# A graph layer, a linear-attention mix and a feed-forward part: four input buffers for the node tiles, slot numbers read early, source terms ahead of the sums

## The chip, the cores and the metric

The kernel runs on one core of a Trainium2 chip. The metric is device time in microseconds (us). Before the change it is 3642.68 us, the median of 3 runs (3634.11 to 3653.83).

## The reference

For 6250 nodes with 256 features, and 206,250 edges sorted by destination:

```python
xn = layernorm(x)
# graph attention, H=8 heads of D=32, T=4 edge types, F=16 edge features
feat_src = (xn @ W_n).reshape(N, H, D)
el = einsum('nhd,hdt->nht', feat_src, attn_l); er = einsum('nhd,hdt->nht', feat_src, attn_r)
em = einsum('ef,hft->eht', edge_attr_16, attn_m)
e = leaky_relu((el[src] . mask + er[dst] . mask + em . mask) / 3)      # mask = edge_attr_4, summed over t
a = exp(e - segment_max(e, dst)[dst]);  a = a / segment_sum(a, dst)[dst]
rst = segment_sum(feat_src[src] * a, dst)
# linear attention over all nodes
q, k, v = split(xn @ Wqkv);  q = softmax(q, over features) * scale;  k = softmax(k, over nodes)
mix = layernorm(((k^T v) q) @ Wout) * gamma
x = x + rst + mix
# 8 experts: router weights from the mean over the nodes, two hidden layers with batch norm and relu
x = x + ffn(layernorm(x))
```

## The kernel before, in words

All arithmetic that matters here is float32. The engines run in parallel and wait for one another by semaphores; the order of work on each engine is written out by hand. Names: PE is the matrix engine, DVE, ACT and POOL work on vectors, SP only issues transfers; transfers from one queue are issued in the order of the code. A register load (`value_load`) reads a number from memory into a register of the engine's sequencer, which then addresses a buffer or sets the value of a wait.

**The node part** (`phase_nodes`, from L108) takes the nodes in 49 tiles of 128. The helper `tiles` (L89) writes the first five steps out, then lets a hook run (`between`), and then either loops over pairs of tiles or, with `unrolled=True`, writes the rest out. A stage given with a lag works on an earlier tile in the same step. Its stages are:

1. Norm and node projection, about 11 to 200 us. SP loads a tile of x into `xin` (`load_x`, L242; two buffers, and from the third tile on it waits until `xn` of two tiles before is out). The load of tile 1 is followed by four tables of the edges' destinations (808 KB each) and the groups' first nodes. DVE takes statistics (`measure`, L434) and one tile later makes `xn` (`norm`, L441), with ACT making the standard deviation in between. PE transposes `xn` (L605), ACT copies it to `xq`, PE projects it (L618), ACT copies the result into `trow`, and POOL stores this row of the table in memory (`store_table`, L331). After tile 4 DVE derives the tables of the edge part (`edge_tables`, L449), 29.75 to 38.7 us. Once all 49 loads are issued SP issues the late weights (L271), the source indices `pidx`, the stores of the derived tables (L277 to L284) and 11 small stores for the table of visits (L286 to L291), most of them of 4-byte elements, one to a partition.
2. Projection to q, k and v, 223 to 345 us, PE bound. ACT copies the results (L403 to L405), DVE keeps the maximum of k. Meanwhile POOL gathers rows of the table for the first edges (`gather_ahead`, L346: 8 gathers of 128 rows each, then the store of the group). It does so for PRE_FIRST = 8 groups, waits for the maximum of k (L361), reduces it (L362), and gathers on up to PRE = 22 groups.
3. The context matrix and the mixed weights (345 to 425), then the mix itself, tile by tile (425 to 560). SP reloads x (`reload`) and stores the result (`store_mix`, L305). DVE runs `measure_out` (L563) for one tile and `finish` (L570) for the tile before, in each step `finish` first.

**The edge part** (`phase_edges`, from L694; about 580 to 2662 us) goes over the edges in K = 125 steps of two visits. A visit is a group of 1024 edges (8 chunks of 128) against one tile of 128 destination nodes. POOL gathers the source rows of a group into one of GSLOTS = 7 slots; which slot a visit uses is a number in memory (`vslot`), and how many groups must have landed is another (`vready`). `pairs` (L777) runs the steps, five written out, then a loop, then the last ones and some beyond the end, in which what is left of the last visits is done. What is done for step k:

- SP (L850) loads the inputs of step k+4 and stores the accumulators of the visits of step k-2, first visit ahead of the loads, second behind.
- PE (L1213): `turn_logits(k)` (L1178, transposes of e), one-hot turn of visit 0 of step k+1 (L1141), `edge_terms(k+1)` (L1149 and L1154, into ps_z), segment sums of visit 0 of step k-1 (L1201), the three register loads `slots_of(k+1)` (L1161, L1162), one-hot turn of visit 1, five chunks of the sums of visit 1, `turn_maxima(k)` (L1188), the other three chunks, `source_terms(k+1)` (L1168, into ps_z, after a wait for the gathered rows).
- DVE (L1083): `logits(k)` (L998: ps_z times the mask), the check for absent segments (`absent`), `over_terms` (L1006, the sum over t), the maxima of the visits, `leak` (L1012, gives e), new maxima of the accumulators (L1033, L1037), `messages(k-1)` for both visits (L1050 register load, L1053 multiply), two scans for the segment maximum (L1061, L1066), `join` of visit 0 of step k-2 (L1044: adds the new sums to the accumulator that ACT has rescaled), the one-hots of step k+2 (L992), `differences(k)` (L1072, L1073), `join` of visit 1.
- ACT takes the segment sums out of PE's buffer (L927), rescales the accumulators (L936) and makes the exponentials.

So ps_z goes from PE to DVE, e back to PE, its transposes to DVE's scans, the scanned maxima back to PE, and their transposes back to DVE.

**The feed-forward part** (`phase_ffn`, 2686 to 3649 us) isn't touched.

## Time and profile before

| what | before |
| --- | --- |
| median of 3 runs | 3642.68 us |
| profiled execution, its own time | 3650.95 us |
| its span | 3649.3 us |
| mean granted clock of TensorE | 0.921 of full |
| PE busy | 84% |
| DVE busy | 74% |
| ACT, POOL busy | 46%, 45% |
| data moved | 486.85 MB, mean 133 GB/s |

PE's busy share is an average: under 70% in most of the node part's slices and over 80% in the edge and feed-forward parts. Busy time is the sum of what the instructions took, so it says nothing of whether they were waited for. In rows of the trace in time, the bracket at the end gives the idle time of the engine ahead of the instruction and what ended it; "issue" is idle time in which the engine waited for nothing that the profile shows. A name with q behind it (DVEq, PEldq) is that engine's sequencer. Matmuls and their weight loads are two rows of one instruction (PE and PEld).

### The profile page before, as it was taken

To read this page: it belongs to the slowest core of one execution; us is meant where nothing else is said; L and a number is where in the kernel's file an instruction comes from. 1 tells how busy PE (TensorE), PEld (TensorE's weight loads), DVE (VectorE), ACT (ScalarE), POOL (GpSimd) and SP (SyncE) were. 2 spreads that over 40 slices of the span, in tenths; PEclk is the share of its full clock that TensorE was granted. 3 is DMA by queue.
4 is the path that set the end of the run, shared out by engine and by line. 5 is a ranking of instruction groups with operands and counts; after the bars stand their busy time and mean duration, and the time that the engine had idled before them with its cause. 6 is when DMAs were issued, how large, how long until landed. Compare 5 with 4: busy or idle time off the path is not lost. (4 is left out here: it accounts for less than half of the span.)

```text
span 3649.3 us, 78668 instructions
## 1 busy us (share of the span) xinstructions
PE 3076.3 (84%) x21479; PEld 2467.3 (68%) x21480; DVE 2687.0 (74%) x5071; ACT 1685.7 (46%) x5779; POOL 1632.3 (45%) x1744
## 2 busy tenths in 40 slices
PE   5469664888888888888888888888849999999999
PEld 2245443767676766767676767666637888888888
DVE  3346563888888888888888888888858776777776
ACT  2334221555555555555555555555533333333333
POOL 1144745766666666666766667777500000000000
PEclk7889876999999999999999999999969999999999
DMA  2253775766666666666666666666521000010000
GB/s 98 80 163 109 239 241 162 193 178 190 176 181 180 184 181 179 181 174 184 180 187 174 181 179 182 179 180 184 132 69 56 28 18 19 20 35 19 18 10 14
DMA packets 364693, 486.85 MB, mean 133 GB/s; under 512 B 165873, under 2 KB 268672, under 8 KB 358798
## 3 DMA queue, kind: packets, MB, share of 16 engines
q0 software_dynamic: 88032, 303.93, 29.3%
q1 hardware_dynamic: 276398, 180.19, 17.1%
q14 instruction: 192, 1.57, 0.1%
q8 instruction: 71, 1.16, 0.1%
HBM read 400.20 MB, written 83.68 MB: 133 GB/s over the span
## 5 line engine op out<-in xcount | busy, mean ns | idle before, releaser
L875 POOL DMA_INDIRECT gat<-scratch_table,idx x1440 | 1391.9, 967 | 638.0 <-issue 447.7
L1201 PE MATMUL ps_s<-msg,oh 128*128 128x272 f32 x4000 | 1012.9, 402 | 25.2 <-ACT tmp L927 15.2
L1201 PEld LDWEIGHTS ps_s<-msg,oh 128*128 128x128 f32 x4000 | 734.8, 191 | 160.8 <-ACT tmp L927 22.2
L1053 DVE TENSOR_TENSOR msg<-gat,ps_m 128x2048 f32<-128x2048 f32 x250 | 560.7, 2284 | 91.3 <-issue 91.3
L1457 ACT ACTIVATE h<-ps_h,fsh,fsc 128x512 f32<-128x512 f32 (+1 forms) x416 | 290.8, 750 | 567.1 <-PE ps_h L1642 567.1
L936 ACT ACTIVATE acc<-acc,sc 128x33 f32<-128x33 f32 x2000 | 458.9, 340 | 165.0 <-DVE acc L1044 165.0
L1422 POOL DMA_DIRECT2D out<-y x12 | 9.1, 761 | 927.2 <-DVE y L1597 927.2
L916 ACT CAST oh<-ps_o 128x1024 f32<-128x1024 bf16 x250 | 259.2, 1037 | 353.2 <-PE ps_o L1141 348.1
L927 ACT ACTIVATE tmp<-ps_s,sc 128x33 f32<-128x33 f32 x2000 | 384.4, 304 | 17.2
L1178 PE MATMUL ps_e<-ident,e 128*16 128x128 f32 x1000 | 149.4, 299 | 258.4 <-DVE e L1012 258.4
L1497 DVE CAST h_hi<-h 128x1024 fp32r<-128x1024 f32 (+1 forms) x208 | 137.4, 660 | 241.7 <-ACT h L1457 241.5
L1178 PEld LDWEIGHTS ps_e<-ident,e 128*16 128x16 f32 x1000 | 84.5, 94 | 327.6 <-DVE e L1012 309.1
L1066 DVE TENSOR_TENSOR_SCAN runm<-penr,ps_e 16x1024 f32<-16x1024 bf16 x125 | 284.3, 2275 | 12.8
L1061 DVE TENSOR_TENSOR_SCAN ps_e<-penr,ps_e 16x1024 f32<-16x1024 bf16 x125 | 284.5, 2276 | 2.0 <-PE ps_e L1178 2.0
L921 ACT ACTIVATE sc<-dd 128x16 f32<-128x16 f32 x250 | 60.0, 240 | 414.1 <-DVE dd L1037 400.2
L1499 DVE TENSOR_TENSOR h_lo<-h,h_hi 128x1024 fp32r<-128x1024 f32 (+1 forms) x208 | 242.1, 1164 | 7.1
L1640 PE MATMUL ps_y<-w_hi,h_hi 128*128 128x256 f32 x784 | 219.7, 280 | 1.4 <-DVE y L1597 1.4
L1641 PE MATMUL ps_y<-w_lo,h_hi 128*128 128x256 f32 x784 | 219.6, 280 | 0.0
L1642 PE MATMUL ps_y<-w_hi,h_lo 128*128 128x256 f32 x784 | 219.3, 280 | 0.0
L1149 PE MATMUL ps_z<-bdm,a 128*128 128x256 f32 x500 | 209.1, 562 | 0.0
L352 POOL DMA_INDIRECT stage<-scratch_table,pidx x176 | 173.9, 988 | 77.5 <-issue 51.7
L1141 PE MATMUL ps_o<-identb,ohT 128*128 128x128 bf16 x2000 | 184.4, 246 | 25.7 <-DVE ohT L992 24.2
(191 smaller groups left out, 5437.7 us busy)
## 6 DMA issues: line engine op xcount, KB each, us to landing
d16r<-scratch_dst SPq DMA_DIRECT2D x250, 256.0 KB
scratch_acc<-acc SPq DMA_DIRECT2D x250, 136.0 KB, 2.5
scratch_ahead<-stage POOLq DMA_DIRECT2D x22, 1152.0 KB, 4.9
gat<-scratch_ahead POOLq DMA_DIRECT2D x22, 1152.0 KB
gat<-scratch_table,idx POOLq DMA_INDIRECT x1440
a<-in_a SPq DMA_DIRECT2D x250, 64.0 KB
scratch_table<-trow POOLq DMA_DIRECT2D x49, 144.0 KB, 2.0
am<-scratch_acc SPq DMA_DIRECT2D x12, 544.0 KB, 4.0
```

Source lines behind the costliest of these rows:

```text
L875: pool.indirect_dma_start(out=gat[:, s, c, :], out_offset=None, in_=scr["table_rows"], in_offset=bass.IndirectOffsetOnAxis(ap=idx[:, g * C ...
L916: act.copy(oh[:, s, j, :, :], ps_o[:, 0:C, :]).then_inc(oh_ok, 1)
L927: act.mul(tmp[:, j, cols], ps_s[j][:, cols], sc[:, j, 1, h:h + 1]).then_inc(tmp_ok, 1)
L936: act.mul(acc[:, new, cols], acc[:, old, cols], sc[:, j, 0, h:h + 1]).then_inc(scaled, 1)
L1053: dve.tensor_tensor(m4[:, :, :, 0:DH], gat[:, row_of(at), :, 0:D].rearrange("p a c (h d) -> p (a c) h d", h=H), ps_p.rearrange("p (c j h) ...
L1061: dve.tensor_tensor_scan(ps_e[0:2 * H, 0:GE], penr[:, s, 0:GE], ps_e[0:2 * H, 0:GE], NEG, ALU.add, ALU.max).then_inc(runf_ok, 1)
L1066: dve.tensor_tensor_scan(runm[:, ::-1], penr[:, s, GE:0:-1], ps_e[0:2 * H, GE - 1::-1], NEG, ALU.add, ALU.max).then_inc(runm_ok, 1)
L1178: last = pe.transpose(ps_e[0:2 * H, c * P:(c + 1) * P], e[:, c * 2 * H:(c + 1) * 2 * H], ident[:, :])
L1201: last = pe.matmul(ps_s[j][:, 0:SUMS], oh[:, s, j, c, :], msg[:, 2 * (s % 2) + j, c, :], start=(c == 0), stop=(c == C - 1), skip_group_che ...
L1457: act.activation(hid[:, m, 0:n * P], ps_h[2 * layer + m][:, 0:n * P], ACT.Relu, bias=sh[:, layer, x * KD + m:x * KD + m + 1], scale=sc[:, ...
L1499: dve.tensor_tensor(lo, whole, hi.bitcast(F32), ALU.subtract).then_inc(parts, 1)
L1640: pe.matmul(out, a_hi, b_hi, start=start, stop=False)
```

## The change

In the node part: `xin` gets four buffers, SP loads x tile 0 ahead of the weights, and its loads are written out with the tables, the late weights, the derived tables and the visit stores put between them after tiles 3, 23 and 35. DVE's tiles of that stage are unrolled. `xn` moves to another region of memory. PRE becomes 24 and PRE_FIRST 11. In the mix DVE does `measure_out` ahead of `finish`. In the edge part: DVE reads both slot numbers at the start of a step; `join` of visit 1 moves from the end of step k to step k+1, behind `over_terms`; the stores on SP follow, and DVE and SP run one step more. PE reads its three numbers behind the first one-hot turn and does the source terms right behind the edge terms, ahead of all sums.

```diff
@@ -40,8 +40,9 @@
 K = V // 2
 SLOTS = 4
 GSLOTS = 7
-PRE = 22
-PRE_FIRST = 8
+PRE = 24
+PRE_FIRST = 11
+XB = 4
 BEFORE = 5
 NEG = -1.0e30
 SLOPE = 0.2
@@ -141,8 +142,7 @@
             wcat = early.enter_context(nc.sbuf_tensor("wcat", [P, KD, D + 2 * HT], F32))
             wnT = early.enter_context(nc.sbuf_tensor("wnT", [P, KD, D], F32))
             bd = early.enter_context(nc.sbuf_tensor("bd", [P, KD, 2 * HT], F32))
-            xin = early.enter_context(nc.sbuf_tensor("xin", [P, 2, D], F32))
-            xn = early.enter_context(nc.sbuf_tensor("xn", [P, 2, D], F32))
+            xin = early.enter_context(nc.sbuf_tensor("xin", [P, XB, D], F32))
         mixw = sb("mixw", [P, KD, D])
         qT = sb("qT", [P, 2, KD, P])
         xre = sb("xre", [P, 2, D])
@@ -170,6 +170,7 @@
         qsum = sb("qsum", [P, 2, H])
         qrs = sb("qrs", [P, NT, H])
         pidx = sb("pidx", [P, PRE * C], I32)
+        xn = sb("xn", [P, 2, D])
         stage = sb("stage", [P, 2, C, ROW])
 
         ps_tr = [ps(f"ps_tr{i}", [P, KD, P]) for i in range(2)]
@@ -185,7 +186,7 @@
         pool_step = sem("n_pool_step")
         attn_w = sem("n_attn_w")
         attn_wc = sem("n_attn_wc")
-        x_in = [sem(f"n_x_in{i}") for i in range(2)]
+        x_in = [sem(f"n_x_in{i}") for i in range(XB)]
         stats = sem("n_stats")
         var_ok = sem("n_var_ok")
         std = sem("n_std")
@@ -239,20 +240,13 @@
 
         @block.sync
         def _(sp):
-            def load_x(t, s):
-
-                if later(t):
-                    sp.wait_ge(xn_ok, t - 1)
-                sp.dma_start(xin[:, s, :], io["x"][row_of(t), :, :].rearrange("a p n -> (a p) n")) \
-                    .then_inc(x_in[s], 16)
-                if isinstance(t, int) and t == 1:
-
-                    for dst, name in ((d_em, "dst_em"), (dn_em, "dst_next_em"), (d_lin, "dst_lin"),
-                                      (dp_lin, "dst_prev_lin")):
-                        sp.dma_start(dst[:, :], io[name].rearrange("(p n) -> p n", p=P)).then_inc(dst_in, 16)
-                    sp.dma_start(gf[:, :], io["group_first"].rearrange("(a n) -> a n", a=1).broadcast_to([P, G - 1])) \
-                        .then_inc(dst_in, 16)
-
+            def load_x(t):
+
+                if t >= XB:
+                    sp.wait_ge(xn_ok, t - XB + 1)
+                sp.dma_start(xin[:, t % XB, :], io["x"][t]).then_inc(x_in[t % XB], 16)
+
+            load_x(0)
             sp.dma_start(wnT[:, :, :], io["W_nT"].rearrange("(c p) n -> p c n", p=P)).then_inc(weights_in, 16)
             sp.dma_start(wcat[:, :, 0:D], io["W_n"].rearrange("(c p) n -> p c n", p=P)).then_inc(weights_in, 16)
             sp.wait_ge(zeroed, 1)
@@ -261,12 +255,19 @@
                 for side, name in enumerate(("attn_l", "attn_r")):
                     sp.dma_start(bd[rows, h // 4, HT * side + T * h:HT * side + T * h + T],
                                  io[name][h]).then_inc(blocks_in, 16)
-            tiles(sp, (load_x, 0))
+            for t in range(1, XB):
+                load_x(t)
             late = [
                 (wqkv[:, :, :], io["Wqkv"].rearrange("(c p) n -> p c n", p=P)),
                 (wout[:, :, :], io["Wout"].rearrange("(c p) n -> p c n", p=P)),
                 (gamma[:, :], io["gamma"].rearrange("(a n) -> a n", a=1).broadcast_to([P, D])),
             ]
+            for dst, name in ((d_em, "dst_em"), (dn_em, "dst_next_em"), (d_lin, "dst_lin"), (dp_lin, "dst_prev_lin")):
+                sp.dma_start(dst[:, :], io[name].rearrange("(p n) -> p n", p=P)).then_inc(dst_in, 16)
+            sp.dma_start(gf[:, :], io["group_first"].rearrange("(a n) -> a n", a=1).broadcast_to([P, G - 1])) \
+                .then_inc(dst_in, 16)
+            for t in range(XB, NT // 2):
+                load_x(t)
             for dst, src in late:
                 sp.dma_start(dst, src).then_inc(late_in, 16)
             sp.dma_start(pidx[:, :].rearrange("p (i c) -> p i c", c=C),
@@ -282,6 +283,8 @@
             sp.dma_start(scr["pen"][0:EP].rearrange("(p n) -> p n", p=P), pen[:, :]).then_inc(stored, 16)
 
             sp.dma_start(scr["pen"][EP:EP + 1].rearrange("(p n) -> p n", p=1), pen[0:1, 0:1]).then_inc(stored, 16)
+            for t in range(NT // 2, 3 * NT // 4):
+                load_x(t)
             sp.wait_ge(visits_ok, 1)
             for k in range(VK):
                 for name, src in (("visit_group", gt_i[:, 0, k:k + 1]), ("visit_tile", gt_i[:, 1, k:k + 1]),
@@ -289,6 +292,8 @@
                                   ("visit_ready", slot[:, 1, k:k + 1])):
                     sp.dma_start(scr[name][k * P:(k + 1) * P].rearrange("(p a) -> p a", a=1), src).then_inc(stored, 16)
             sp.dma_start(scr["group_visit"].rearrange("(a n) -> a n", a=1), gb_i[0:1, :]).then_inc(stored, 16)
+            for t in range(3 * NT // 4, NT):
+                load_x(t)
 
             sp.wait_ge(er_step, 5)
             sp.dma_start(scr["er"].rearrange("t p n -> p t n"), er3[:, :, :]).then_inc(stored, 16)
@@ -432,8 +437,8 @@
         @block.vector
         def _(dve):
             def measure(t, s):
-                dve.wait_ge(x_in[s], (t - s) * 8 + 16)
-                dve.bn_stats(st[:, s, :], xin[:, s, :]).then_inc(stats, 1)
+                dve.wait_ge(x_in[t % XB], (t // XB + 1) * 16)
+                dve.bn_stats(st[:, s, :], xin[:, t % XB, :]).then_inc(stats, 1)
                 dve.wait_ge(stats, t + 1)
                 settle(dve)
                 dve.bn_aggr(mv[:, s, :], st[:, s, :]).then_inc(var_ok, 1)
@@ -444,7 +449,7 @@
                 dve.wait_ge(rstd_ok, t + 1)
                 if later(t):
                     dve.wait_ge(turn_ps, t - 1)
-                dve.tensor_scalar(xn[:, s, :], xin[:, s, :], mv[:, s, 0:1], rstd[:, s, 0:1],
+                dve.tensor_scalar(xn[:, s, :], xin[:, t % XB, :], mv[:, s, 0:1], rstd[:, s, 0:1],
                                   ALU.subtract, ALU.mult).then_inc(xn_ok, 1)
 
             def edge_tables():
@@ -484,7 +489,7 @@
                 dve.wait_ge(step, 12 + VK)
                 dve.tensor_tensor(slot[:, 0, :], gt_i[:, 0, :], quot[:, :], ALU.subtract).then_inc(visits_ok, 1)
 
-            tiles(dve, (measure, 0), (norm, 1), between=edge_tables)
+            tiles(dve, (measure, 0), (norm, 1), between=edge_tables, unrolled=True)
 
             def heads(t):
                 return xq[:, row_of(t), :].rearrange("p a (h d) -> p (a h) d", h=H)
@@ -582,7 +587,7 @@
                 dve.scalar_tensor_tensor(mixf[:, s, :], mixo[:, s, :], rstd[:, s, 0:1], xre[:, s, :],
                                          ALU.mult, ALU.add).then_inc(mixf_ok, 1)
 
-            tiles(dve, (finish, 1), (measure_out, 0))
+            tiles(dve, (measure_out, 0), (finish, 1))
 
         @block.tensor
         def _(pe):
@@ -846,14 +851,14 @@
                 loads(k, k)
 
             def step(k, s):
-                if not known(k, 2):
-                    store(k - 2, s % 2, 0)
+                if not known(k, 3):
+                    store(k - 3, (s + 1) % 2, 1)
                 if not (isinstance(k, int) and k + SLOTS >= K):
                     loads(k + SLOTS, s)
-                if not known(k, 2):
-                    store(k - 2, s % 2, 1)
-
-            pairs(sp, step, 2)
+                if not (known(k, 2) or isinstance(k, int) and k >= K + 2):
+                    store(k - 2, s % 2, 0)
+
+            pairs(sp, step, 3)
             for i in range(4):
                 sp.wait_ge(acc_out[i], 16 * len(range(i, V, 4)))
 
@@ -1044,10 +1049,13 @@
                 dve.tensor_tensor(acc[:, 2 * q + j, 0:H * HW], acc[:, 2 * q + j, 0:H * HW], tmp[:, j, :],
                                   ALU.add).then_inc(acc_ok, 1)
 
-            def messages(k, s, j):
+            def slot_of(k, j):
+
+                return dve.value_load(vslot[0:1, row_of(k * 2 + j)], min_val=0, max_val=GSLOTS - 1)
+
+            def messages(k, s, j, at):
 
                 b = 2 * (s % 2) + j
-                at = dve.value_load(vslot[0:1, row_of(k * 2 + j)], min_val=0, max_val=GSLOTS - 1)
                 dve.wait_ge(p_ok, k * 2 + 1)
                 m4 = msg[:, b, :, 0:H * HW].rearrange("p c (h w) -> p c h w", w=HW)
                 dve.tensor_tensor(m4[:, :, :, 0:DH],
@@ -1081,8 +1089,10 @@
             def step(k, s):
 
                 alive = not (isinstance(k, int) and k >= K)
-                merging = not known(k, 2)
+                merging = not (known(k, 2) or isinstance(k, int) and k >= K + 2)
                 w, q = k - 2, s % 2
+                if not known(k, 1) and not (isinstance(k, int) and k > K):
+                    at = [slot_of(k - 1, j) for j in range(2)]
                 if alive:
                     logits(k, s)
                 if merging:
@@ -1091,6 +1101,8 @@
                     old_maximum(w, q, 0, small_a)
                 if alive:
                     over_terms(k)
+                if not known(k, 3):
+                    join(k - 3, 1 - q, 1)
                 if merging:
                     dve.wait_ge(small_a, w * 3 + 2)
                     dve.wait_ge(small_b, w * 3 + 1)
@@ -1109,8 +1121,8 @@
                     dve.wait_ge(max_ok, w * 2 + 2)
                     below_new_maximum(q, 1)
                 if not known(k, 1) and not (isinstance(k, int) and k > K):
-                    messages(k - 1, (s - 1) % SLOTS, 0)
-                    messages(k - 1, (s - 1) % SLOTS, 1)
+                    messages(k - 1, (s - 1) % SLOTS, 0, at[0])
+                    messages(k - 1, (s - 1) % SLOTS, 1, at[1])
                 if alive:
                     scans(k, s)
                 if alive:
@@ -1121,10 +1133,8 @@
                     select(k + 2, (s + 2) % SLOTS)
                 if alive:
                     differences(k, s)
-                if merging:
-                    join(w, q, 1)
-
-            pairs(dve, step, 2)
+
+            pairs(dve, step, 3)
 
         @block.tensor
         def _(pe):
@@ -1221,11 +1231,12 @@
                     pe.wait_ge(in_[s1], loaded(k + 1, s1))
                     pe.wait_ge(ohT_ok, k * 2 + 4)
                     turn_one_hot(k + 1, s1, 0)
+                    at, groups = slots_of(k + 1)
                     edge_terms(k + 1, s1)
+                    source_terms(at, groups)
                 if summing:
                     segment_sums(k - 1, s0, 0, range(C))
                 if more:
-                    at, groups = slots_of(k + 1)
                     turn_one_hot(k + 1, s1, 1)
                 if summing:
                     segment_sums(k - 1, s0, 1, range(0, BEFORE))
@@ -1233,8 +1244,6 @@
                     turn_maxima(k, s)
                 if summing:
                     segment_sums(k - 1, s0, 1, range(BEFORE, C))
-                if more:
-                    source_terms(at, groups)
 
             pairs(pe, step, 2)
 
```

## Rows read from the trace of the kernel before

**Rows 1.** busy us of engines by stage, then granted clock, DMA share, GB/s
```profile
11.00:200.00 189.00, 101.73 (x307) 56.48 (x307) 61.81 (x214) 56.32 (x198) 25.66 (x47) 0.82 0.30 97
...
425.00:511.00 86.00, 48.41 (x160) 35.14 (x158) 39.24 (x126) 17.34 (x53) 60.40 (x66) 0.76 0.93 297
...
601.00:2646.00 2045.00, 1758.62 (x14855) 1416.77 (x14856) 1701.61 (x2961) 1146.16 (x4647) 1384.07 (x1441) 0.93 0.65 179
```

**Rows 2.** L1178 (turn_logits): duration ns, first and last start, its idle time
```profile
L1178 PE MATMUL ps_e<-ident,e x1000: 272/273/422, 601.6 to 2646.1; 128*16 128x128 f32 x167
...
  DVE e L1012: 567.5, 250
```

**Rows 3.** PE in time, step at full clock: start, us, instruction, idle before
```profile
1576.09 1.04 PE L1178 MATMUL ps_e<-ident,e 128*16 128x128 f32 x8 [2.07 <-DVE e L1012]
...
1577.41 1.08 PE L1149 MATMUL ps_z<-bdm,a 128*128 128x256 f32 x4
...
1580.09 3.93 PE L1201 MATMUL ps_s<-msg,oh 128*128 128x272 f32 x16 [0.40 <-ACT tmp L927]
1583.85 0.61 PE L1141 MATMUL ps_o<-identb,ohT 128*128 128x128 bf16 x8
...
1586.87 0.64 PE L1188 MATMUL ps_m<-ident,runm 16*128 16x16 f32 x8
...
1588.91 1.03 PE L1168 MATMUL ps_z<-gat,ident 128*128 x4
1592.01 0.28 PE L1178 MATMUL ps_e<-ident,e 128*16 128x128 f32 x1 [2.07 <-DVE e L1012]
```

**Rows 4.** PE in time, a step whose clock falls
```profile
1509.82 1.36 PE L1178 MATMUL ps_e<-ident,e 128*16 128x128 f32 x8 [2.11 <-DVE e L1012]
...
1511.83 2.02 PE L1149 MATMUL ps_z<-bdm,a 128*128 128x256 f32 x4
```

**Rows 5.** the slice in which those edge terms run, columns as above
```profile
1511.00:1512.00 1.00, 1.00 (x10) 1.00 (x9) 0.61 (x1) 1.00 (x7) 0.00 (x0) 0.50 0.65 189
```

**Rows 6.** DVE in time, at the end of that step
```profile
1522.24 0.29 DVE L1072 TENSOR_TENSOR dlt<-e,ps_m 128x128 f32<-128x128 f32 x1 [0.36 <-PE ps_m L1188]
...
1523.03 0.43 DVE L1044 TENSOR_TENSOR acc<-acc,tmp 128x264 f32<-128x264 f32 x1 [0.31 <-ACT acc L936]
1524.67 0.69 DVE L998 TENSOR_TENSOR zm<-ps_z,a 128x512 f32<-128x512 f32 x1 [1.21 <-PE ps_z L1168]
...
1526.30 0.35 DVE L1012 SCALAR_TENSOR_TENSOR e<-lg 128x64 f32<-128x64 f32 x2
...
1528.16 4.49 DVE L1053 TENSOR_TENSOR msg<-gat,ps_m 128x2048 f32<-128x2048 f32 x2 [0.65 <-issue]
```

**Rows 7.** register loads on DVE (L1050): ns min/median/max, first and last start
```profile
L1050 DVEq FUSED_REGOPS  x424: 53/190/210, 621.9 to 2662.1; - x142
L1050 DVEq TENSOR_LOAD <-vslot x250: 300/303/553, 621.3 to 2661.8; - x125
```

**Rows 8.** register loads on PE (L1161): ns min/median/max, first and last start
```profile
L1161 PEldq TENSOR_LOAD <-vslot x250: 294/302/496, 584.7 to 2634.1; - x125
```

**Rows 9.** statistics and norm of a node tile in time
```profile
104.40 0.43 DVE L436 BATCH_NORM_STATS2 st<-xin 128x6 f32<-128x256 f32 x1 [2.25 <-DMA xin<-in_x]
...
105.33 0.41 DVE L447 TENSOR_SCALAR xn<-xin,mv,rstd 128x256 f32<-128x256 f32 x1
...
107.98 0.43 DVE L436 BATCH_NORM_STATS2 st<-xin 128x6 f32<-128x256 f32 x1 [2.24 <-DMA xin<-in_x]
```

**Rows 10.** waits of 0 to 560 us: total us, times, longest
```profile
DVE st L436 <- DMA xin<-in_x: 121.6, 47, 11.4
...
POOL kmaxb L362 <- DVE kmax L500: 41.9, 1, 41.9
...
DVE mixf L582 <- DMA scratch_xmix<-mixf: 33.3, 21, 4.0
```

**Rows 11.** the first copy of a projection on ACT, in time
```profile
222.68 0.37 ACT L403 COPY ktile<-ps_qk 128x256 f32<-128x256 f32 x1 [22.44 <-DMA scratch_group_visit<-gb_i]
```

## The prediction, made before the changed kernel was run

> **What bounds the kernel now.** I read the busy times by stage first. The kernel has three parts: nodes (to 580 us), edges (580 to 2662), and a feed-forward part that the change leaves alone. [Rows 1]: in the edge stage PE is busy 86% of 2045 us, DVE 83%, POOL 68%, so no engine is full and the order of work decides. The lines from 11 to 200 show PE half idle and the DMA engines at 0.30, while from 425 to 511 the DMA engines are at 0.93: the nodes are bound by waits first and by transfers later. One wait stands out on PE, in the view of the line that ends it [rows 2]: turn_logits (L1178) sat idle 567.5 us until DVE's e (L1012), matmuls and weight loads counted together, at the start of each step. The 1000 matmuls of that line run from 601.6 to 2646.1, 125 steps with the last one's own 1 us behind, a mean of 16.48 us a step.
>
> The steps in order of time show the ring. E is the time at which e is ready, just before L1178. At full clock [rows 3] PE goes from E over one-hot, edge terms (L1149 at +1.32), sums, one-hot, five chunks of sums, maxima (L1188 at +10.78), three chunks and the source terms (L1168, +12.82). DVE then turns ps_z into e, and the next L1178 starts at +15.92. [Rows 4] is the same ring when the clock has fallen: L1149 takes 2.02 where it took 1.08, at a granted clock of 0.50 [rows 5], the lower level of 1.2 GHz, and the step, from 1509.82 to the e of [rows 6] at 1526.30 and 0.40 on, is 16.88. [Rows 6] shows DVE: differences (L1072) as soon as the maxima are out, join (L1044), then 1.21 us idle until ps_z, logits (L998), e 1.63 later, messages (L1053) after an idle 0.65 put down to "issue". That is the register load of a slot number: [rows 7], 0.303 for the load, with its register operations 0.67 us in all (two lines of 0.19 and a check beside it).
>
> **The edges, part by part.** What the change wants: source terms right behind the edge terms, so that ps_z is there long before DVE asks, and no join in front of the logits. What it pays is read from where register loads stand. In the new place they follow one short one-hot turn, and the edge terms are behind them. The only cover is turn_logits and the one-hot, 1.32 us [rows 3].
> - E to L1149: 0.3 of waits, 2.2 of loads and a start, 2.75 (now 1.32): **+1.43**.
> - Edge terms 2.2 and source terms 0.87, both from [rows 3] with their overlap taken off: the source terms move from behind the maxima to ahead of them, **+0.87** on the way to the maxima, and 10 us nearer to POOL, which is 68% busy and so has slack.
> - Sums 3.76 (the 0.40 wait for ACT goes), one-hot and five chunks 3.02, maxima to the start of differences 0.60. Maxima done: 2.75 + 2.2 + 0.87 + 3.76 + 3.02 + 0.6 = **E + 13.2**.
> - DVE from there: now differences, join, wait, logits. In the new order the two loads of slot numbers stand ahead of the logits, behind differences: 2 x 0.67 from its start on is 1.34, and with what surrounds them logits start at +1.48, where the two short operations of differences (0.29 for the first) alone would let them start at 0.44. Logits to e is 1.63 + 0.40 to the start of L1178 [rows 6]; the join of the second visit (0.36 net) is now inside this stretch, ahead of leak. 1.48 + 2.03 + 0.39 = 3.9. The three last chunks of sums on PE (1.5) lie beside it.
> - Step: 13.2 + 3.9 = **17.1** at full clock, against 15.92 at full clock and 16.48 in the mean. Messages start 0.65 earlier, which nobody waits for: DVE's own work in a step is 13.6 us of 16.4 [rows 1].
> - Clock: PE now idles twice in each ring (1 us behind the one-hot, 2.4 ahead of L1178), so I expect the half-clock stretch in nearly all steps, but mostly over that idle time and the transposes, where it costs little: 0 added, with 0.6 (the rival R1) as the other end.
> 121 full steps, of the 125, x (17.1 - 16.48) = **+75 us**. What hid the loads was a long run of matmuls; that cover is gone. What SP's new order of stores moves is off the path: the store of a second visit goes one step later, and four accumulator buffers are there for it. One more step at the tail and an early wait for POOL: **+3**.
>
> Whether PE's edge terms can enter the queue while a load runs is the dearest unknown; the ends are 0 and +1.43 there, and on DVE 0 and 1.04 more. I take the upper ends for the row that is nearest: an idle 0.65 before L1053 on DVE, though its inputs were there [rows 6]. Beside it stands the Trainium skill, "Advanced Engine Details and Errata", on the sequencer and instruction queues: other engine instructions can be read and queued while microcode executes. By that rule the loads would cost nothing in either place and the step be under 16; the 0.65 speaks against it here.
>
> **The nodes.** One tile of the first stage [rows 9]: statistics at 104.40 after 2.25 us of waiting for the DMA of x, the next at 107.98, so 3.5 a tile. xin has two buffers and its load waits for xn of two tiles before. Four buffers and unrolled loads hide it. All 49 statistics waited 121.6 us in all [rows 10]. The new tile lies between 1.34 (DVE from statistics to the end of xn, [rows 9]) and 2.08 (PE's busy 101.73 by 49, [rows 1], with overlapping records and a clock of 0.82). PE and DVE alternate over two tile buffers; I take 1.75, nearer to the middle. 44 tiles are 77 us. The first five and the edge tables end at about 34 instead of 40, since x's tiles are no longer behind four tables of 808 KB: 111. The late weights and derived tables (L271 to L284, some 3 MB) now stand in the middle of the x loads. By the 297 GB/s of [rows 1] they are 10 us, of which the four buffered tiles hide some: +7. The visit stores, tiny elements, hold up the writes of others: today ACT waits 22.44 for the last and starts the projections at 222.68 [rows 11]. The same block of writes stays, now in the middle of the stage, where the table stores of two tiles cover a part: +16 of it kept, between 0 and 22, and 2 for the last tile. 111 + 7 + 16 + 2 = 136: **-87**. The ends are -55 (a tile of 2.5) and -105 (1.35).
>
> PRE 24 and PRE_FIRST 11: POOL waited 41.9 us for kmax (L362, [rows 10]). A group is 8 gathers and a store, and 66 POOL instructions took 86 us [rows 1], so 11.7 a group; three more are 35 and fit there. Later 13 groups stand beside the mix instead of 14. There the DMA engines are the bound (0.93, [rows 1]), with 33.3 us waiting for the store of the mix [rows 10] in 86: one group of 11.7 us fewer gives back about 4. Measure ahead of finish gives DVE something to do in that wait: 3, between 0 and 6. **-7**.
>
> **Sum.** -87 - 7 + 75 + 3 = -16. The profiled execution took 3650.95 (span 3649.3), 8 above the median of 3642.68; on the median: **3626**.
>
> **Rivals.**
> R1, slower: the half-clock stretch falls on edge terms and sums in each step. Then to 17.1 come 0.6 of the 0.95 that L1149 loses [rows 3, 4], the rest of it lying over idle, 17.7: 121 x 1.22 = +148, less 91, some 3700. The mean of 16.48 lies 0.4 of the way back from 16.88 to 15.92. For the rival: in some three steps of five the clock fell behind the 2.07 of idle, and on L1149 [rows 4]. Against it: in the other two it stayed up behind the same idle. It decides from a step of 17.23 up, where the 91 us of gain (87 + 7 - 3) are used up. The Trainium skill, "TensorE: Matmul & The Clock Gate", says in its part on the PE-mode transpose that a transpose doesn't count as PE work in the same way for the clock; more of the ring's first part would then be idle in its eyes, and the time be this rival's.
> R2, the loads are hidden (queued work passes them, or they overlap what I counted after them): PE's ring loses the 2.07 by about 1, steps of 15.8: 121 x -0.68 = -82, with the nodes 3642.68 - 94 - 82 + 3 = 3470. Against it: the 0.65 of [rows 6].
> R3, the first stage isn't freed: PE at half clock bounds it at 2.5 a tile, 44 x 0.75 = +33 and we get 3659: no change to slightly slower.
>
> **How the numbers follow.** Main case 0.55, half of it under 3624.5 by the spread of the tile and step terms (0.1 us a step is 12 us). R1 0.19, R2 0.13, R3 0.13. 0.5% is 18 us, about what a measurement can tell from no change. Faster: 0.13 + 0.28 + a little from cases between the main one and R2 = 0.43. Slower by over 18 us: R1 and a corner of R3 = 0.22. Same 0.35. The range reaches from 3580 (a step of 16.75) to 3695 (just short of R1): about 2 in 10 lie outside, R2 and the far end of R1. The main case's own range is 3600 to 3655.
>
> **What the profile after would show.** Right: ACT's wait of 22.4 gone; statistics' wait 121.6 down to 25 to 40; the first projection copy at about 136; POOL's wait for kmax near 0; the edge stage from about 490. In a step: PE idle about 1 before L1149's successor, put down to "issue"; about 2.4 before L1178's; DVE idle 1 before logits, by "issue", and none before the messages; a period of 17.0 to 17.2. Wrong: a period under 16.5 (loads hidden) or over 17.23; DVE waiting for ps_z; POOL's gathers releasing PE; statistics still waiting for x.

## The result, and the profile after

The changed kernel takes 3685.2 us (median of 4 runs, 3682.4 to 3689.6) against 3640.6 for the kernel before (4 runs, 3634.1 to 3653.8, among them the three known ahead of the prediction). The ratio is 1.0119, with a 95% interval of 1.0088 to 1.0150. It was forecast at 3626, faster; it is slower by about 45 us. The time lies inside the stated range, but on the other side of no change.

The profiled execution of the changed kernel has a span of 3688.0 us, 38.7 more than before. These are the times at which some of PE's matmuls start, in us of the profiled executions. The last column is the changed node part alone, which is explained below.

| point in the kernel | before | after | node part alone |
| --- | --- | --- | --- |
| last matmul of the first stage | 197.9 | 150.8 | 150.8 |
| last projection to q and k | 345.4 | 276.2 | 276.2 |
| mix, first to last | 421.5 to 556.4 | 353.5 to 522.4 | 353.7 to 482.8 |
| edges, turn_logits first to last | 601.6 to 2646.1 | 567.2 to 2689.6 | 527.6 to 2571.8 |
| end | 3649.3 | 3688.0 | 3572.5 |

So the first stage gave 69 us up to the last projection, the mix took 34 of them back, and the edge part took 78 more. What follows the edges was 5 us shorter.

**The node part.** First the waits of the changed kernel up to 152 us (total us, times, longest).

```profile
POOL scratch_table L339 <- ACT er_f L397: 121.2, 43, 24.7
...
ACT trow L396 <- DMA scratch_table<-trow: 54.4, 30, 24.0
DVE rstd L448 <- ACT rstd L383: 53.6, 31, 24.0
DVE st L441 <- DMA xin<-in_x: 26.4, 5, 8.1
```

The wait of the statistics for x is 26.4 where it was 121.6 [rows 10]. What ends last is now ACT's wait until the table store of two tiles before has landed, and one of its 30 waits is 24.0 us long. The rows of ACT and of SP in time show where that is:

```profile
96.74 0.37 ACT L389 COPY xq<-ps_tr 128x256 f32 x1 [0.16 <-PE ps_tr L610]
121.11 0.40 ACT L396 COPY trow<-ps_ft 128x288 f32<-128x288 f32 x1 [24.00 <-DMA scratch_table<-trow]
```

```profile
73.68 20.68 SPq L247 DMA_DIRECT2D xin<-in_x  x12
94.41 0.42 SPq L293 DMA_DIRECT2D scratch_visit_group<-gt_i  x1
...
112.71 0.29 SPq L294 DMA_DIRECT2D scratch_group_visit<-gb_i  x1
113.05 29.33 SPq L247 DMA_DIRECT2D xin<-in_x  x13
```

The small visit stores are issued from 94.41 on, and from 97.1 to 121.1 ACT, and with it the whole first stage, stands still: the stores of the table don't land. The two issued at 95.80 and 96.90 took 25.29 and 24.51 us, where the median of the 49 is 2.3:

```profile
DMA to landing us min/median/max: 2.0/2.3/25.3
```

The first copy of the projections is at 153.98, not at 136, against 222.68 before [rows 11].

**The mix.** PE and DVE, two tiles in time, in the changed kernel:

```profile
424.16 2.04 PE L685 MATMUL ps_v<-mixw,qT 128*128 128x256 f32 x4 [0.84 <-DVE mixo L578]
426.00 0.63 PE L677 MATMUL ps_tr<-ident,xq 128*128 128x128 f32 x2
427.52 2.05 PE L685 MATMUL ps_v<-mixw,qT 128*128 128x256 f32 x4 [0.89 <-DVE mixo L578]
```

```profile
426.24 0.43 DVE L570 BATCH_NORM_STATS2 st<-ps_v 128x6 f32<-128x256 f32 x1 [1.64 <-PE ps_v L685]
426.78 0.18 DVE L573 BATCH_NORM_AGGREGATE mv<-st 128x2 f32<-128x6 f32 x1
426.89 0.48 DVE L578 SCALAR_TENSOR_TENSOR mixo<-ps_v,mv,gamma 128x256 f32<-128x256 f32 x1
...
427.75 0.48 DVE L587 SCALAR_TENSOR_TENSOR mixf<-mixo,rstd,xre 128x256 f32<-128x256 f32 x1 [0.31 <-DVE rstd L581]
```

These are two engines taking turns. DVE waits 1.64 us for PE's tile (measure_out), and only behind it may it read the tile before out of PE's buffer (mixo, in finish). PE waits 0.89 for that read before it starts the next tile. In the windows of 353 to 426 and 426 to 523 us the granted clock is 0.55 and 0.50 (the last columns are clock, DMA share and GB/s):

```profile
353.00:426.00 73.00, 47.57 (x122) 31.75 (x120) 31.16 (x94) 12.99 (x41) 54.84 (x60) 0.55 0.91 293
426.00:523.00 97.00, 71.47 (x173) 46.66 (x171) 45.20 (x145) 16.17 (x57) 1.46 (x2) 0.50 0.31 99
```

**The edges.** A step of the changed kernel on PE and the end of it on DVE. E, the time at which e is ready and turn_logits starts, is at 1511.48; the next one is at 1528.58.

```profile
1511.48 1.88 PE L1188 MATMUL ps_e<-ident,e 128*16 128x128 f32 x8 [2.30 <-DVE e L1017]
...
1524.06 0.67 PE L1198 MATMUL ps_m<-ident,runm 16*128 16x16 f32 x8
...
1528.58 1.04 PE L1188 MATMUL ps_e<-ident,e 128*16 128x128 f32 x8 [2.29 <-DVE e L1017]
1529.46 0.61 PE L1151 MATMUL ps_o<-identb,ohT 128*128 128x128 bf16 x8
1531.18 1.13 PE L1159 MATMUL ps_z<-bdm,a 128*128 128x256 f32 x4 [1.11 <-issue]
...
1533.35 1.11 PE L1178 MATMUL ps_z<-gat,ident 128*128 x4
```

```profile
1524.76 0.29 DVE L1080 TENSOR_TENSOR dlt<-e,ps_m 128x128 f32<-128x128 f32 x1 [2.05 <-PE ps_m L1198]
...
1526.17 0.69 DVE L1003 TENSOR_TENSOR zm<-ps_z,a 128x512 f32<-128x512 f32 x1 [0.92 <-issue]
```

PE stands 1.11 us ahead of the edge terms and DVE 0.92 ahead of the logits (1.45 in the step after). Both are put down to "issue", so the engine waited for nothing that the profile shows. In PE's gap its sequencer was loading the numbers (`slots_of`, L1171):

```profile
L1171 PEldq TENSOR_LOAD <-vslot x2: 302/302/302, 1529.0 to 1529.8; - x2
```

Before, neither gap existed, and the only such gap was 0.65 ahead of the messages [rows 6], where there is none now. The mean step, from the first to the last turn_logits as in [rows 2], is 17.11 us. The line of turn_logits sat idle longer than the 567.5 of [rows 2]:

```profile
L1188 PE MATMUL ps_e<-ident,e x1000: 272/277/421, 567.2 to 2689.6; 128*16 128x128 f32 x167
...
  DVE e L1017: 661.3, 250
```

The first of the two E shown has a fallen clock (turn_logits takes 1.88), the second has not (1.04). Over the 118 steps in the middle of the edge stage, the granted clock fell somewhere in 84 steps of the changed kernel and in 76 of the kernel before. The steps in which it stayed up took 16.83 and 15.93 on average, the others 17.18 and 16.73.

### The profile page after: what moved, and what is told of

The parts are those of the page before. It is cut to its first block and busy times, and to the rows that moved or that the text cites. A ratio compares the mean times of both kernels' runs of the same rounds, so it can differ in the third digit from the quotient of the medians.

```text
span 3688.0 us, 78275 instructions
## 1 busy us (share of the span) xinstructions
PE 3071.0 (83%) x21479; PEld 2441.9 (66%) x21480; DVE 2674.3 (73%) x5071; ACT 1679.0 (46%) x5779; POOL 1635.7 (44%) x1748
## 3 DMA queue, kind: packets, MB, share of 16 engines
q1 hardware_dynamic: 276654, 180.20, 17.1%
q8 instruction: 72, 1.18, 0.2%
## 5 line engine op out<-in xcount | busy, mean ns | idle before, releaser
L1211 PE MATMUL ps_s<-msg,oh 128*128 128x272 f32 x4000 | 1001.1, 398 | 5.3 <-ACT tmp L932 5.3
L1211 PEld LDWEIGHTS ps_s<-msg,oh 128*128 128x128 f32 x4000 | 742.5, 191 | 144.7 <-DVE msg L1061 6.2
L1188 PE MATMUL ps_e<-ident,e 128*16 128x128 f32 x1000 | 176.7, 337 | 303.9 <-DVE e L1017 303.9
L1188 PEld LDWEIGHTS ps_e<-ident,e 128*16 128x16 f32 x1000 | 95.3, 105 | 391.1 <-DVE e L1017 357.3
L1159 PE MATMUL ps_z<-bdm,a 128*128 128x256 f32 x500 | 153.8, 433 | 77.0 <-issue 76.7
L357 POOL DMA_INDIRECT stage<-scratch_table,pidx x192 | 187.8, 978 | 62.3 <-issue 56.2
L1080 DVE TENSOR_TENSOR dlt<-e,ps_m 128x128 f32<-128x128 f32 x125 | 36.0, 288 | 236.4 <-PE ps_m L1198 236.4
```

The lines of the kernel that those rows point to most:

```text
L1188: last = pe.transpose(ps_e[0:2 * H, c * P:(c + 1) * P], e[:, c * 2 * H:(c + 1) * 2 * H], ident[:, :])
L1211: last = pe.matmul(ps_s[j][:, 0:SUMS], oh[:, s, j, c, :], msg[:, 2 * (s % 2) + j, c, :], start=(c == 0), stop=(c == C - 1), skip_group_che ...
```

## The experiments

The theory after this reading: the change is three pieces that don't touch one another. The node part gives about 70 us; the new order in the mix takes 34; the register loads at their new places, and the join ahead of e, take 78. Twelve kernels were run, each in rounds beside the kernel before, whose median was 3652 to 3654 us there; the changed kernel's own ratio is against 3641.

| kernel | time, us | ratio to before, 95% interval | mean step |
| --- | --- | --- | --- |
| changed kernel | 3685 | 1.0119 [1.0088, 1.0150] | 17.11 |
| changed, old mix order | 3653 | 1.0001 [0.9988, 1.0014] | 17.11 |
| before, new mix order | 3684 | 1.0076 [1.0054, 1.0099] | 16.49 |
| changed nodes, old mix order, old edges | 3576 | 0.9790 [0.9765, 0.9816] | 16.48 |
| before, changed edges | 3732 | 1.0211 [1.0188, 1.0234] | 17.09 |
| changed, old mix, DVE's loads back | 3565 | 0.9756 [0.9736, 0.9775] | 16.38 |
| changed, old mix, PE's order of before | 3647 | 0.9980 [0.9970, 0.9991] | 17.10 |
| changed nodes, PE's loads hoisted alone | 3651 | 0.9996 [0.9986, 1.0006] | 17.09 |
| changed nodes, source terms behind the maxima | 3478 | 0.9522 [0.9502, 0.9542] | 15.69 |
| changed, old mix, source terms early but loads covered | 3473 | 0.9511 [0.9489, 0.9533] | 15.66 |
| source terms behind the maxima, absent late | 3487 | 0.9557 [0.9535, 0.9578] | 15.76 |
| the same, and the join late | 3420 | 0.9364 [0.9342, 0.9387] | 15.26 |
| changed nodes, visit stores last | 3574 | 0.9798 [0.9774, 0.9821] | 16.48 |

### The three pieces alone

The old order of the mix in the changed kernel:

```diff
-            tiles(dve, (measure_out, 0), (finish, 1))
+            tiles(dve, (finish, 1), (measure_out, 0))
```

> The changed kernel, with finish ahead of measure_out again in the mix. Theory: in the new order DVE waits for the matmuls of tile t before it finishes tile t-1, and PE waits for that finish before it may start tile t+1, so both stand in one ring of 3.43 us a tile. Then the mix falls from 169 us to about 135 and the time from 3685 to about 3648. Rival: the mix became longer since 24 groups of gathers and a fallen clock share its time; then the order gives under 8 us and the time is 3677 or more.

Measured: 3653, ratio 1.0001, where the changed kernel has 1.0119. The mix runs from 359.1 to 492.1, 133 us. The longest waits of that stretch are again those of the kernel before, with the store of the mix among them:

```profile
ACT rstd L433 <- DVE mv L573: 87.7, 47, 12.0
...
PE ps_v L685 <- ACT qT L429: 52.7, 30, 12.5
DVE mixf L587 <- DMA scratch_xmix<-mixf: 29.5, 19, 4.1
```

The reverse edit in the kernel before:

```diff
-            tiles(dve, (finish, 1), (measure_out, 0))
+            tiles(dve, (measure_out, 0), (finish, 1))
```

> The kernel before, with the new order of the mix alone. Theory (one ring through DVE and PE): the mix goes from 135 to about 169 us, and the time from 3641 to about 3675. Rival (the order matters only with the other parts): within 8 us of 3641.

Measured: 3684, +0.76%, 30 us; the mix takes 167 us. It holds with none of the other parts present, under the gathers (a granted clock of 0.54 up to 510 us) and without them (0.50 behind). The rival, contention with the gathers, falls: by PE's instructions, six a tile, a tile takes 3.5 us in the first window and 3.3 in the second, where POOL and the DMA engines are nearly idle.

```profile
427.00:510.00 83.00, 55.93 (x141) 37.48 (x141) 36.49 (x114) 14.57 (x48) 60.63 (x67) 0.54 0.94 293
510.00:594.00 84.00, 61.92 (x151) 40.60 (x149) 39.01 (x125) 13.87 (x49) 1.47 (x2) 0.50 0.32 103
```

What these runs don't separate is the order itself and the clock. In both kernels with the new order the clock stayed at about 0.50 to the end of the mix; with the old order it rose again in the second half (0.88 in the kernel before from 511 to 560 us, 0.91 in the run above from 430 to 493). The tiles of the kernel before from 528 us on ran at full clock:

```profile
529.99 1.10 PE L680 MATMUL ps_v<-mixw,qT 128*128 128x256 f32 x4 [0.69 <-ACT qT L424]
...
531.90 1.10 PE L680 MATMUL ps_v<-mixw,qT 128*128 128x256 f32 x4 [0.59 <-ACT qT L424]
```

There a tile takes 1.96 us, and its four matmuls 1.10 where the new order has 2.04. With 0.94 less in each of 48 steps, the 169 us of the changed kernel's mix would be 124, an estimate, and that is less than the 129 to 135 of the old order. So the two engines do take turns, but by this estimate the 34 us are lost only because the clock stays down as well. That it stays down went with the new order in every run; no run had the new order at full clock.

The node part of the change with the old mix order, and the old edge part (the hunks of the change ahead of the edge part, less the one on the mix):

> The changed node part (four input buffers, loads spread, 24 and 11 groups gathered ahead), with the old order in the mix and the edge part of before. Theory: the first stage ends 71 us earlier than before and nothing later takes that away: 3641 - 71 = 3570, between 3560 and 3578. Rival: a part of it is given back where POOL's gathers and the mix meet, 3590 or more.

Measured: 3576, ratio 0.979. The profile's points are in the first table: 69 us earlier at the last projection, 74 at the end of the mix. Nothing is given back.

The edge part of the change in the kernel before (its other hunks, from SP's stores on):

> The kernel before with the changed edge part alone. Theory: a step takes 17.1 us in place of 16.48, as in the changed kernel, and the time is 3641 + 78 less a few for the tail: 3710 to 3722. Rival: the edge part of the changed kernel was slow in part because it began with other groups gathered ahead; then the step is under 16.9 and the time under 3695.

Measured: 3732, 2.1% more, 17.09 us a step. That is 10 over the range, which was reckoned from 3641; the kernel before took 3654 beside this run, and the difference is 78. The clock fell in 107 of the 118 middle steps. Nodes and edges add: -2.1% and +2.1% make 0, and the changed kernel with the old mix order measured 1.0001. The mix order costs +0.8% in the kernel before and +1.2% in the changed one, 30 to 43 us; the profiles have 32 and 34 to 40 for it.

### What in the edges costs

DVE's register loads back in front of the messages, PE as changed:

```diff
-                if not known(k, 1) and not (isinstance(k, int) and k > K):
-                    at = [slot_of(k - 1, j) for j in range(2)]
...
-                    messages(k - 1, (s - 1) % SLOTS, 0, at[0])
-                    messages(k - 1, (s - 1) % SLOTS, 1, at[1])
+                    messages(k - 1, (s - 1) % SLOTS, 0, slot_of(k - 1, 0))
+                    messages(k - 1, (s - 1) % SLOTS, 1, slot_of(k - 1, 1))
```

> The changed kernel with the old mix order, and DVE's register loads of slot numbers back in front of the messages; PE as changed. Theory (a register load holds up the instructions behind it unless a long one runs ahead): the two loads no longer stand between differences and logits, logits start 1.04 us sooner in each step, 17.11 becomes about 16.1, the edge part 2122 becomes 2000 and the time about 3530. Rival (DVE's loads run while something else is waited for, and only PE's cost): the step stays over 16.9, the time over 3630.

Measured: 3565 and 16.38 a step. The direction is the theory's and the size is 0.7 of it. Of the 0.73 us that a step lost, about 0.5 is the loads' and the rest the clock's: the clock now stays up in all steps (1.00 from 601 to 2500 us, where it was 0.96), and the steps in which it had stayed up took 16.89 before this edit, where all take 16.35 now. Logits now start 0.41 behind differences instead of 1.41. But over_terms, which came 0.89 behind the start of logits, comes 1.41 behind it:

```profile
1515.17 0.29 DVE L1080 TENSOR_TENSOR dlt<-e,ps_m 128x128 f32<-128x128 f32 x1 [1.01 <-PE ps_m L1196]
...
1515.58 0.68 DVE L1003 TENSOR_TENSOR zm<-ps_z,a 128x512 f32<-128x512 f32 x1
...
1516.74 0.17 DVE L1025 TENSOR_SCALAR absn<-ps_s 128x8 f32<-128x8 f32 x1 [0.41 <-PE ps_s L1209]
...
1516.99 0.68 DVE L1011 TENSOR_REDUCE lg<-zm 128x128 f32<-128x512 f32 x1
```

Between the two stands `absent`, whose second half needs the last sum, and that sum ends on PE at 1516.70 (the run that starts at 1515.06 and takes 1.64). It became the next wait.

PE's order of before, with DVE's early loads and later join:

```diff
-                    at, groups = slots_of(k + 1)
                     edge_terms(k + 1, s1)
-                    source_terms(at, groups)
                 if summing:
                     segment_sums(k - 1, s0, 0, range(C))
                 if more:
+                    at, groups = slots_of(k + 1)
                     turn_one_hot(k + 1, s1, 1)
...
                     segment_sums(k - 1, s0, 1, range(BEFORE, C))
+                if more:
+                    source_terms(at, groups)
```

> The changed kernel with the old mix order, and PE's order of before; DVE's early loads and later join stay. Theory: with the source terms late, DVE's loads (1.34 behind the start of differences) end before ps_z is there (2.43 behind it) and cost nothing; the join, now ahead of e, adds 0.36: a step of 16.85, an edge part of 2090, the time about 3620. Rival (DVE's two loads cost wherever they stand): 1 us more, 17.8 a step, about 3740.

Measured: 3647, 17.10 a step, so 0.25 over the theory. DVE's loads do cost nothing here, since DVE waits 1.95 for ps_z anyway. The join, ahead of e, makes PE's idle time 2.41 instead of 2.07, and the granted clock between 601 and 2500 us is 0.90 instead of 0.93: turn_logits takes 1.87 where it took 1.04 and 1.36 in [rows 3] and [rows 4]. The clock fell in all 118 middle steps, where it fell in 77 of the kernel with the changed nodes alone.

```profile
1520.17 1.03 PE L1178 MATMUL ps_z<-gat,ident 128*128 x4
1523.60 1.87 PE L1188 MATMUL ps_e<-ident,e 128*16 128x128 f32 x8 [2.41 <-DVE e L1017]
1525.27 1.06 PE L1151 MATMUL ps_o<-identb,ohT 128*128 128x128 bf16 x8
```

```profile
1521.23 0.69 DVE L1003 TENSOR_TENSOR zm<-ps_z,a 128x512 f32<-128x512 f32 x1 [1.95 <-PE ps_z L1178]
```

PE's register loads alone, ahead of the edge terms:

```diff
+                    at, groups = slots_of(k + 1)
                     edge_terms(k + 1, s1)
                 if summing:
                     segment_sums(k - 1, s0, 0, range(C))
                 if more:
-                    at, groups = slots_of(k + 1)
                     turn_one_hot(k + 1, s1, 1)
```

> The changed node part with the old mix order and the old edge part, but PE's three register loads behind the first one-hot turn, ahead of the edge terms; source terms stay at the end. Theory: the loads uncovered cost PE's ring 0.9 to 1.4 a step, against 16.48: 17.4 to 17.9, the time 3690 to 3750. Rival (other instructions are queued while a load runs, so it costs nothing): 16.5 a step and 3576.

Measured: 3651, 17.09 a step: 0.61 more than 16.48, so the loads do cost, and less than the 0.9 to 1.4 expected. The edge terms start 2.73 behind E, as the sum had it, but the clock had fallen by then, and turn_logits and the one-hot take 1.77 and 1.06:

```profile
1502.50 1.77 PE L1183 MATMUL ps_e<-ident,e 128*16 128x128 f32 x8 [2.10 <-DVE e L1017]
1504.06 1.06 PE L1146 MATMUL ps_o<-identb,ohT 128*128 128x128 bf16 x8
1505.23 1.52 PE L1154 MATMUL ps_z<-bdm,a 128*128 128x256 f32 x4
```

At half clock they cover most of the loads. The 0.61 has two parts of about the same size. With the clock fallen in both, a step takes 17.07 against 16.74 in the kernel without this edit, so the loads cost 0.3. The rest is that the clock now falls in all 118 middle steps and not in 77 of them, though PE's idle time ahead of turn_logits is 2.07 in both.

### Source terms early, loads covered

This keeps the idea of the change (source terms ahead of the maxima, the join behind over_terms) and leaves the loads beside long work. DVE's stand in front of the messages again. On PE, against the order of before (the line of the source terms at the end of the step goes):

```diff
                 if summing:
                     segment_sums(k - 1, s0, 0, range(C))
                 if more:
                     at, groups = slots_of(k + 1)
                     turn_one_hot(k + 1, s1, 1)
+                    source_terms(at, groups)
```

> The changed kernel with the old mix order, with the source terms early still, but under the cover of work: behind the one-hot turn of visit 1, the register loads of PE in their old place beside the sums of visit 0, those of DVE in front of the messages. Theory: what made the change slow was where the register loads stand, not the early source terms; 0.95 more on the way to the maxima, 1.25 less behind them, and an idle PE under 1.8, at which the clock stayed up in the two runs that had it: 15.6 a step, the time about 3470. Rival (source terms ahead of the maxima cost what they save): 16.3 a step as with the loads of PE uncovered, the time about 3560.

Measured: 3473, 15.66 a step. It is 180 us under the changed kernel with the old mix order (3653), and the difference between the two is only where the loads stand, and how early the source terms are. Some 0.2 of the 1.45 us a step are the clock's, which no longer falls. PE's idle time before turn_logits is 1.78, and the step has no fallen clock.

The same gain from a one-place edit of the old edge part:

```diff
                 if alive:
                     turn_maxima(k, s)
+                if more:
+                    source_terms(at, groups)
                 if summing:
                     segment_sums(k - 1, s0, 1, range(BEFORE, C))
-                if more:
-                    source_terms(at, groups)
```

> The changed node part with the old mix order and the old edge part; PE does the source terms behind the transposes of the maxima, ahead of the last three chunks of sums, register loads where they were. Theory: what DVE waits for is ps_z and then the last sum; ps_z comes 1.5 us sooner without lengthening the way to the maxima, and the last sum 0.9 later becomes the next end of a wait: a step of about 15.7, the time about 3480. Rival (the last sum is the bound already, and is now 0.9 later): 16.9 or more a step, the time over 3620.

Measured: 3478, 15.69 a step, as expected. DVE no longer waits for ps_z in the rows of its steps.

Two steps further: the check for absent segments and the group maximum of the second visit behind leak.

```diff
-                    absent(w, 1, small_b)
                     old_maximum(w, q, 0, small_a)
...
-                    dve.wait_ge(small_b, w * 3 + 1)
                     group_maximum(0, small_a)
-                    group_maximum(1, small_b)
                 if alive:
                     leak(k)
                 if merging:
+                    absent(w, 1, small_b)
                     dve.wait_ge(small_a, w * 3 + 3)
                     new_maximum(w, q, 0)
                     dve.wait_ge(max_ok, w * 2 + 1)
+                    dve.wait_ge(small_b, w * 3 + 1)
+                    group_maximum(1, small_b)
                     old_maximum(w, q, 1, small_b)
```

> The kernel whose source terms stand behind the maxima's transposes (15.69 a step, 3478 us), with the check for absent segments and the group maximum of the second visit moved behind leak, so that e no longer waits for the last sum of the step before. Theory: PE idles 1.74 behind that last sum because DVE's chain to e starts at it; freed, e comes 0.5 to 0.9 sooner: 14.8 to 15.2 a step, the time 3365 to 3420. Rival (the join's wait for ACT, 0.76, or DVE's own loop sets e anyway): over 15.5 a step and over 3455.

Measured: 3487, 15.76 a step. The theory failed and its rival holds. DVE's logits were held up by the join in front of them, which waits 0.76 for ACT's rescaling, and that didn't change:

```profile
1521.64 0.28 DVE L1077 TENSOR_TENSOR dlt<-e,ps_m 128x128 f32<-128x128 f32 x1
1521.84 0.28 DVE L1078 TENSOR_TENSOR msg<-ps_m,dme 128x128 f32<-128x128 f32 x1
1522.88 0.43 DVE L1049 TENSOR_TENSOR acc<-acc,tmp 128x264 f32<-128x264 f32 x1 [0.76 <-ACT acc L941]
1523.23 0.68 DVE L1003 TENSOR_TENSOR zm<-ps_z,a 128x512 f32<-128x512 f32 x1
```

With that join behind leak as well (and SP's stores and the extra step of the change):

```diff
                 if alive:
                     leak(k)
+                if not known(k, 3):
+                    join(k - 3, 1 - q, 1)
                 if merging:
                     absent(w, 1, small_b)
...
                     differences(k, s)
-                if merging:
-                    join(w, q, 1)
```

> The same, and the join of the second visit moved behind leak too, into the next step, so that logits wait for ps_z alone. Theory: logits start about 0.4 sooner than with the join ahead of them, but the join's 0.36 goes into DVE's loop ahead of the messages: 14.6 to 15.0 a step, the time 3345 to 3400. Rival (DVE's loop is the bound, so the place of the join is worth nothing): equal to the kernel with the join in its old place, within 10 us.

Measured: 3420, 15.26 a step (the middle one is 15.02), 68 us under the run before it, so the place of the join is worth a lot once the last sum is out of the way; the rival falls. Whether the join alone would have paid wasn't tried. The time missed its range by 20 us. PE's idle time before turn_logits is 0.60, where it was 1.66. It is the fastest kernel of the study, 6.4% under the kernel before.

### The stall of the visit stores

In the kernel with the changed node part alone:

```diff
-            sp.wait_ge(visits_ok, 1)
-            for k in range(VK):
...
             for t in range(3 * NT // 4, NT):
                 load_x(t)
+            sp.wait_ge(visits_ok, 1)
+            for k in range(VK):
...
```

> The changed node part with the old mix order and the old edge part (3576 us), with the eleven small visit stores behind all loads of x, as before the change. Theory: in the changed kernel the one stall of 24 us in the first stage is theirs; now that stage ends at about 128 instead of 151, but the projections wait about 22 us for the stores: 3576 within 8. Rival (the stall has another cause, as the store of the table or the loads): the first stage still ends near 151, and the wait of 22 us comes on top: 3595 or more.

Measured: 3574, the same time as with the stores in the middle. Half of the theory fails: the first stage still ends at 151.2. SP's loads run four tiles ahead, so the stores are issued from 117.02 on, inside the stage, and ACT waits 9.56 and 14.80 us for the table's stores, 24.4 in all:

```profile
129.12 0.40 ACT L396 COPY trow<-ps_ft 128x288 f32<-128x288 f32 x1 [9.56 <-DMA scratch_table<-trow]
...
144.96 0.40 ACT L396 COPY trow<-ps_ft 128x288 f32<-128x288 f32 x1 [14.80 <-DMA scratch_table<-trow]
```

The stall moved with the stores, so it is theirs, at 22 to 27 us in three places: 22.44 before [rows 11]; 24.00 in the changed kernel, 16.6 and 9.1 in the one with its nodes alone, 16.5 and 10.9 in the one with the old mix order; and 24.4 here. In the kernel before, it was the last small store that ACT waited for, and the two table stores issued at 200.01 and 200.80 took 18.93 and 19.11 us to land. Why eleven small stores hold up others for so long wasn't tried.

## Why the prediction failed

**Edges: the sum right, by some luck.** Forecast 17.1 a step and +75; measured 17.11 and +78. The gaps came where they were forecast, and the edge terms start at +2.60 where 2.75 was. But 17.1 was forecast at full clock, with nothing for the clock. At full clock the step is 16.83, 0.27 shorter, and the clock adds about as much again. In the step shown above, E to the end of the maxima is 13.25 (1511.48 to 1524.73), with turn_logits at half clock; in the step after it, at full clock, it is 12.93 (1528.58 to 1541.51), against 13.2. From the end of the maxima to the next E it was 3.9 and is 3.85 and, with 1.45 of "issue" on DVE, 4.35. Against the kernel before, the change costs 0.90 a step at full clock (16.83 against 15.93), where 1.18 was forecast; and of the 0.56 that the clock cost a step before, all was forecast to go and half did. The two errors cancel.

The traces don't agree with the rule of the Trainium skill, "Advanced Engine Details and Errata", Sequencer Loop, that other instructions can be queued while microcode executes: behind the register loads PE stood 1.11 us and DVE 0.92, both put down to "issue". R2 falls with it.

The half-clock stretch didn't come in nearly all steps, but in 84 of 118, at a granted clock of 0.96 between 601 and 2500 us, up from 0.93. R1 falls: in the kernel before with the changed edge part the clock fell in 107 of 118 steps, and the step was 17.09, not 17.7. The transposes ahead of the edge terms didn't bring the clock down in the kernels with 1.78 of idle, so the rule on transposes of the Trainium skill, "TensorE: Matmul & The Clock Gate", PE-mode transpose, decided nothing that these runs can tell.

**First stage: right in kind, 18 short.** Forecast -87, measured -69 (153.98 against 222.68). The tile was 1.75 in the forecast. The 39 tiles behind the sixth and outside the two stalls took 70.0, so 1.79, and the first copy comes 5.9 behind the last xn where 2 was taken. The late tables cost 9 where 7 was taken. The term that was mis-sized most is the stall of the visit stores, "+16 of it kept", 10 of the 18: it cost 26 to 27 (xn of two tiles 30 us apart less the two tiles' own 3.6). I thought the stage's own work would run beside it, but the stage stores a table tile every 1.8 us into two buffers, so it stops after two.

**Mix order: the step that failed.** "Measure ahead of finish gives DVE something to do in that wait: 3, between 0 and 6" was forecast as a gain of 3; it is a loss of 32 to 40 us of the mix in the profiles, and of 30 to 43 in the runs. I priced it as DVE's order alone, in the face of a wait of DVE for a DMA. What I didn't ask is the question that I asked of the edges: who waits for what is queued behind the new wait. finish(t-1) frees the buffer for PE's tile t+1; behind measure_out(t) it can't run until PE's tile t is done, so two buffers work as one. No rival named this mechanism, and no end of a range held it. A tile takes 3.34 us so, with its matmuls at half clock, and would take 2.40 by the estimate above if the clock had come back; the prediction said nothing of the clock in the mix. How much of the loss is each one's stays open. Without it the other terms are -69 (forecast -87), -4 in the mix (-4), +78 (+75) and -5 (+3). They make 0, where -13 was forecast, and 3653 against 3654 was measured.

The gathers ahead: POOL stood idle 41.9 for kmax [rows 10] and now 5.8, put down to "issue", and with the old order the mix took 129 us instead of 135.

So one step had the wrong sign and was off by 41 us (-7 for the mix and the gathers, +34 in the profile), and one was short by 18. With 3 more for the edges, 8 less for the tail and 1 of rounding they turn -16 into the +39 of the profiled executions.

## What to carry to other kernels

When two operations of one engine swap places, follow the one that is now second: which buffer does it free, and does the engine that waits for that buffer also feed the one that is now first? If so, double buffering is gone and the two engines take turns; look at the granted clock of that stretch too, before the whole loss is put down to the turns. A register load was free here only where long work of the same engine ran ahead of it, or where the engine waited for something later anyway. Hoisting it "early" can be the dearest place. And an early result is worth only the distance to the next wait: the source terms early, the late check and the late join paid together, while the check alone paid nothing. And a sum that comes out right to 3 us can hold two errors of a quarter of a us a step each: compare steps at the same clock.

## What the runs showed of the hardware

- TensorE's granted clock in the edges stayed at 1.00 (2.4 GHz, 601 to 2400 us) in the kernels in which PE idled 1.6 to 1.9 us ahead of turn_logits, also where a second gap of 1.1 to 1.2 follows. In the one with 0.60 it fell in 4 of 118 steps. With 2.07 and more it fell, but the idle time alone doesn't order these kernels: 0.93 at 2.07, 0.90 at 2.07 with the register loads behind the one-hot, 0.96 and 0.94 at 2.2 to 2.8 with a second gap of 1.1, and 0.90 at 2.41, where it fell in each step.
- In the mix with its new order PE idled 0.84 to 0.89 us in each tile of 3.34 us, and the clock was at 0.50 (1.2 GHz) from 371 us to the end. From 528 us on in the kernel before, with the old order, it idled 0.59 to 0.69 in each tile of 1.96, and the clock was at full.
- Three register loads on PE ahead of the edge terms cost 0.61 us a step and not 0.9 to 1.4: about half of it at an equal clock, the other half because the clock fell in more of the steps.
- Eleven stores of small elements held up other stores in all three places: single stores of the table took 19 to 28 us to land, where the median is 2.0 to 2.3.
